# Graph attention, edge stage: GpSimd weighs one head of every pair of visits behind its gathers, TensorE lowers addresses ahead of its waits

## The reference

```python
Q, K, V = (x @ Wq), (x @ Wk), (x @ Wv)            # each reshaped to (N, 8 heads, 64)
score = jnp.einsum('ehd,ehd->eh', K[src], Q[dst]) / sqrt(64)
score = jnp.exp(jnp.clip(score, -5.0, 5.0))[..., None]
wV = segment_sum(V[src] * score, dst)
Z = segment_sum(score, dst)
h = x + (wV / (Z + 1e-06)).reshape(N, 512)
h = (h - mean(h)) * rsqrt(var(h) + 1e-05) * bn_gamma + bn_beta     # over the nodes
out = layernorm(x + h)                                            # over the features
```

## Time and profile before

| | us |
|---|---|
| three runs | 1913.06, 1907.57, 1913.44 |
| median | 1913.06 |
| the profiled execution | 1908.01 |
| its span in the trace | 1906.1 |

### The profile page before, as it was taken

One profiled execution on the slowest core, in us unless ns is written; L12 is line 12 of the kernel. 1 busy time (PEld: TensorE's weight loads), 2 busy tenths in 40 slices (PEclk: granted clock), 3 DMA queues, 4 the chain that ended last, 5 costly groups with the idle time before them and its releaser, 6 DMA issues.

```text
span 1906.1 us, 41424 instructions
## 1 busy us (share of the span) xinstructions
PE 1861.6 (98%) x7904; PEld 1362.2 (71%) x8014; DVE 1697.0 (89%) x2454; ACT 1367.5 (72%) x4602; POOL 1291.3 (68%) x1473
## 2 busy tenths in 40 slices
PE   7999999998999999999999999999999999999897
PEld 4555555554888888878888888888888888887333
DVE  6677755644999999999999999999999999999888
ACT  0002000002999999999999999999999999998857
POOL 0205666103777888788888888888888888885677
PEclk9999999999999999999999999999999999999999
DMA  5547788546999999999999999999999999999307
GB/s 183 162 151 250 288 319 274 186 161 231 357 358 356 362 367 358 346 351 368 368 356 353 352 366 369 354 355 355 366 361 358 360 355 365 370 358 370 122 33 287
DMA packets 184521, 589.09 MB, mean 309 GB/s; under 512 B 28480, under 2 KB 30240, under 8 KB 184480
## 3 DMA queue, kind: packets, MB, share of 16 engines
q0 software_dynamic: 135904, 465.14, 65.8%
q1 hardware_dynamic: 45120, 121.69, 17.8%
q10 hardware_dynamic: 3456, 1.78, 0.3%
HBM read 535.27 MB, written 78.91 MB: 322 GB/s over the span
## 4 chain that ended last, share of the span: by engine, by line
PE 74%; DVE 16%; issue 4%; DMA 4%; ACT 1%; POOL 1%; SPq 0%; DVEq 0%; ACTq 0%; POOLq 0%
PE acc L939 29%; PE places L342 22%; PE q_ps L923 17%; DVE kv L795 6%; DVE raw L806 5%; DMA kv<-kv_d,idx 2%; PE mm_ps L949 2%; PE banks L1151 1%; DVE stats L1288 1%; DVE agg L1281 1%; PE mm_ps L951 1%; PE places L402 1%; DMA q_tile<-xb_d 1%; POOL kv L751 1%; PE banks L1142 1%
## 5 line engine op out<-in xcount | busy, mean ns | idle before, releaser
L751 POOL DMA_INDIRECT kv<-kv_d,idx x880 | 887.0, 1008 | 339.2 <-issue 204.8
L846 ACT ACTIVATE kv<-kv 128x64 f32<-128x64 f32 x3520 | 889.0, 335 | 14.3
L939 PE MATMUL acc<-kv,mm_sb 128*128 128x260 f32 x3520 | 845.6, 383 | 4.1 <-POOL kv L714 2.2
L939 PEld LDWEIGHTS acc<-kv,mm_sb 128*128 128x128 f32 x3520 | 654.3, 190 | 137.9 <-issue 32.8
L923 PE MATMUL q_ps<-q_tile,mm_sb 128*128 x1760 | 559.2, 439 | 5.6 <-DVE kv L795 4.9
L795 DVE TENSOR_TENSOR kv<-q_ps,kv 128x1024 f32<-128x1024 f32 x440 | 536.1, 1218 | 14.0 <-PE q_ps L923 7.0
L806 DVE TENSOR_REDUCE raw<-kv 128x16 f32<-128x1024 f32 x440 | 532.2, 1210 | 0.0
L923 PEld LDWEIGHTS q_ps<-q_tile,mm_sb 128*128 128x128 f32 x1760 | 328.6, 189 | 74.4 <-DVE kv L795 20.8
L714 DVE TENSOR_TENSOR kv<-kv 128x384 f32<-128x384 f32 (+1 forms) x440 | 271.6, 617 | 0.1
L857 ACT ACTIVATE mm_sb<-mm_ps,less 128x1024 fp32r<-128x1024 f32 x220 | 241.2, 1096 | 13.1 <-remote 10.1
L435 ACT COPY p<-places 128x768 f32<-128x768 f32 x23 | 18.4, 798 | 243.5 <-PE places L342 243.5
(11 more groups left out here) (171 smaller groups left out, 1358.6 us busy)
## 6 DMA issues: line engine op xcount, KB each, us to landing
q_tile<-q_d SPq DMA_DIRECT2D x49, 512.0 KB, 7.2
kv<-kv_d,idx POOLq DMA_INDIRECT x880, 6.2
kv_d<-kv_a SPq DMA_DIRECT2D x25, 512.0 KB, 5.5
xb<-in_x POOLq DMA_DIRECT2D x49, 256.0 KB, 4.3
xb_d<-xb POOLq DMA_DIRECT2D x49, 256.0 KB, 3.7
out_rows<-agg SPq DMA_DIRECT2D x49, 256.0 KB, 2.1
x_sb<-in_xT SPq DMA_DIRECT2D x24, 512.0 KB, 7.9
q_d<-q_a SPq DMA_DIRECT2D x24, 512.0 KB, 4.1
```

The lines of the kernel that those rows point to most:

```text
L751: pool.indirect_dma_start(kv[:, s, u, 0:2 * DIM], None, kv_d, bass.IndirectOffsetOnAxis(idx[:, s, u:u + 1], 0), bounds_check=N_NODES - 1, ...
L846: return act.activation(v, v, ACT.Copy, scale=kv[:, s, u, 2 * DIM + h:2 * DIM + h + 1])
L939: last = pe.matmul(acc[:, bass.ds(par, 1), DIM - (1 - n) * HALF:DIM + n * HALF], m, kv[:, sc, u, DIM + n * HALF:DIM + (n + 1) * HALF], sta ...
```

## The change

Three things, all in `attend`:

1. GpSimd weighs head 7 of **every** pair, and in two instructions, one for each visit (`weigh_visit`, 64 values a partition). The first stands behind the gather of visit 0 (and behind the copy of row numbers, where there is one), the second behind the gather of visit 1. The wait for the exponentials, on `s_exp` of the pair five back, stands ahead of the first.
2. VectorE weighs three heads of every pair, none of four, and TensorE waits for three counts on `s_v` in every step.
3. TensorE's program works out the addresses of all four Q matmuls, and of all four sums, ahead of the waits in front of them (`pe.lower_ap`), as well as the values that `s_q` and `s_evict` are awaited with. In `follow`, `& 1` is written `% 2`.

```diff
-                return (mask >> k) & 1
+                return (mask >> k) % 2
...
+        def weigh_visit(eng, s, u):
+
+            first = HEADS - POOL_HEADS
+            v = kv[:, s, u, DIM + first * D_HEAD:2 * DIM]
+            w = kv[:, s, u, 2 * DIM + first:KVW].broadcast_to([P, D_HEAD])
+            return eng.tensor_tensor(v, v, w, ALU.mult)
...
+                if there(p):
+                    wait_apart(pool, s_exp[sp], fp)
+                    weigh_visit(pool, sp, 0)
                 if there(q):
                     gather(q, s, fills, 1)
-                if s % 2 and there(p):
-                    wait_apart(pool, s_exp[sp], fp)
-                    weigh(pool, sp, HEADS - POOL_HEADS, POOL_HEADS).then_inc(s_v[sp], 1)
+                if there(p):
+                    weigh_visit(pool, sp, 1).then_inc(s_v[sp], 1)
...
-                    weigh(dve, s2, ACT_HEADS, HEADS - ACT_HEADS - (POOL_HEADS if s % 2 == 0 else 0)).then_inc(s_v[s2], 1)
+                    weigh(dve, s2, ACT_HEADS, HEADS - ACT_HEADS - POOL_HEADS).then_inc(s_v[s2], 1)
...
+                    loaded = pe.snap(16 * (tiles[1] + 1), min_val=16, max_val=16 * TILES)
+                    parts = [q_tile[:, bass.ds(tiles[u] % 2, 1), n * DIM:(n + 1) * DIM].bitcast(F32R)
+                             for u in range(2) for n in range(2)]
+                    for part_q in parts:
+                        pe.lower_ap(part_q)
                     pe.wait_ge(s_mm[sb_ // 2], fb)
-                    pe.wait_ge(s_q, 16 * (tiles[1] + 1))
+                    pe.wait_ge(s_q, loaded)
                     for u in range(2):
                         for n in range(2):
-                            part_q = q_tile[:, bass.ds(tiles[u] % 2, 1), n * DIM:(n + 1) * DIM].bitcast(F32R)
+                            part_q = parts[2 * u + n]
...
-                    pe.wait_ge(s_v[sc], (2 if sc % 2 else 3) * fc)
-                    pe.wait_ge(s_evict, tiles[1] + 1)
+                    sums = [acc[:, bass.ds(tiles[u] % 2, 1), DIM - (1 - n) * HALF:DIM + n * HALF]
+                            for u in range(2) for n in range(2)]
+                    emptied = pe.snap(tiles[1] + 1, min_val=1, max_val=TILES)
+                    for part in sums:
+                        pe.lower_ap(part)
+                    pe.wait_ge(s_v[sc], 3 * fc)
+                    pe.wait_ge(s_evict, emptied)
```

More of the change, by code:

```diff
@@ L932, in step @@
                              for u in range(2)]
-                    pe.wait_ge(s_v[sc], (2 if sc % 2 else 3) * fc)
-                    pe.wait_ge(s_evict, tiles[1] + 1)
+                    sums = [acc[:, bass.ds(tiles[u] % 2, 1), DIM - (1 - n) * HALF:DIM + n * HALF]
[5 more added lines that the diff above has]
+                    pe.wait_ge(s_evict, emptied)
                     for u in range(2):
-                        par = tiles[u] % 2
                         m = one_hot(sc, u, 0).bitcast(F32)
                         for n in range(2):
-                            last = pe.matmul(acc[:, bass.ds(par, 1), DIM - (1 - n) * HALF:DIM + n * HALF], m,
+                            last = pe.matmul(sums[2 * u + n], m,
                                              kv[:, sc, u, DIM + n * HALF:DIM + (n + 1) * HALF],
```

## The result

The changed kernel takes 2078.57 us (median of four, 2077.04 to 2080.95) against 1910.99 us before (four runs, 1907.57 to 1913.44). The ratio is 1.0879, with a 95% interval of 1.0855 to 1.0904: 168 us slower, 8.8%. The forecast was 1959 us in a range of 1908 to 2000, and the measured time lies outside it. Its direction was right and the size was not: it foresaw 48 us and 168 came.

What follows compares the result with a forecast made beforehand. TensorE and VectorE bound the old kernel by a hair; GpSimd would bound the new one at 3.035 us a pair. (3.035 - 2.926) x 440 = 48 us on 1908.0, plus 3, gives 1959 us, range 1908 to 2000.

Steps and rivals of the forecast that it cites:

- The reading of the bound: Edge stage before: TensorE and VectorE bound by a hair; GpSimd nearly full, with 0.15 us a pair to give.
- the elastic weighing of the earlier trace: GpSimd's old 128-value weighing: 0.41 us undisturbed, mean 0.665, stretched when GpSimd runs ahead until it meets VectorE's weighing.
- The order of the waits: Edge stage after: GpSimd sets the pace, TensorE's sums wait for it, and VectorE's product waits for TensorE.
- the wait for the exponentials costs nothing: GpSimd's new wait in every step: ended long ago when GpSimd is late, so it costs 0.
- The line through 128 and 512 values: GpSimd visit size: 0.41 and 1.28 us give 2.27 ns a value, so 0.265 us for 64; 0.27 taken.
- The other reading that stood in the text: GpSimd visit of 64 values: with the copy's fixed part, near 0.30 us.
- the pauses and the gaps around the copy: GpSimd, per two pairs: pauses 0.04 us; the row-number copy with its gap adds 0.11 us.
- is a gain in itself: GpSimd: placing each visit behind a gather turns a gap of 0.30 into 0.18 us.
- So I take no stretch: GpSimd's visits: VectorE's weighing falls between them, in the second gather, so no stretch is added to 3.015 us a pair.
- The phase: Edge stage after: VectorE weighs about 1.6 to 2.6 us after a second visit's end, during the second gather (1.6 to 2.7).
- a rival of 0.08: GpSimd's visits meet VectorE's weighing and stretch: beyond 2000 us, 2044 with half the pairs caught; chance 0.08.
- TensorE's part: TensorE's address work ahead of the waits: costed at 0, with 3 us of gain or loss either way.

Runs made afterwards that it cites:

- The run with one input: Changed kernel with VectorE's two-input weighing of 3 heads replaced by a one-input reduction over the same 384 values; 1971.11 us, ratio 1.0324.

## Why the prediction was half right

**The reading of the bound held.** GpSimd, 68% busy by the page, had 0.15 us a pair to give and not the 18% of the earlier trace rows: one weighing for every pair, unstretched, took 2.96 us a pair, where GpSimd's own sum gave 2.97. Its idle pieces of 0.16 and 0.02 us stand unchanged around the shorter visits, as costs of an instruction. And the elastic weighing of the earlier trace rows is confirmed: with one input it takes 0.412 us and GpSimd idles instead.

**The order of the waits held**, as did that the wait for the exponentials costs nothing: GpSimd's idle time names ACT for 3.0 of 121.3 us.

**A visit was mis-sized by 0.03.** The line through 128 and 512 values gave 0.265 and I took 0.27; undisturbed it is 0.30. The other reading that stood in the text, a fixed part like that of the copy, was nearer: some 0.19 us. Two visits of a pair by 0.03 are 27 us of the sum. The run with one input, which has this and no stretch, came out at 1971, only 12 above the forecast of 1959; the pauses and the gaps around the copy came out smaller than forecast. That placing each visit behind a gather "is a gain in itself" holds for the gaps alone: the split as a whole cost 50 us.

**The step that failed is "So I take no stretch".** The phase was worked out right for some 60% of the pairs: it had VectorE weigh 1.6 to 2.6 us after the end of a second visit, in the time of the second gather. (In 135 of the 360 pairs in the middle VectorE weighs earlier, from the last part of the first gather on, and stretches neither gather.) In the trace after, a second visit ends at 1000.42, VectorE weighs from 1001.89 (1.47 later), the second gather starts at 1002.09 (1.67 later). But I took a gather to be immune, since no row that I read showed otherwise, and asked only whether a weighing would be caught. So the phase that looked safe was a bad one: the weighing stands on the start of 223 of 360 second gathers, and of nearly every copy. The forecast put the stretch into a rival of 0.08 and priced it for visits alone. The terms that were mis-sized, per pair: gathers 2 x 1.105 = 2.21 against 2.06 (+0.15), visits 0.64 against 0.54 (+0.10, of which 0.06 is the size of a visit above and 0.04 is stretch), the copy 0.12 against 0.05 (+0.07). Together +0.32, less 0.03 for pauses and gaps that came out smaller: 0.29 x 440 = 128 us, against the 120 by which the forecast missed.

A row in the trace before would have told me. These two stand beside each other in its timeline, the gather being the second after the pause in the earlier trace rows:

```profile
1063.47 0.55 DVE L714 TENSOR_TENSOR kv<-kv 128x384 f32<-128x384 f32 x1
...
1063.63 1.25 POOL L751 DMA_INDIRECT kv<-kv_d,idx  x1 [0.30 <-issue]
```

A gather of 1.25 us among hundreds of 0.99, starting inside VectorE's weighing. Only 20 of the 720 gathers in the middle of that stage begin so, and 13 of them take over 1.06 us; with the change 223 do. The pause of the earlier trace rows had pushed GpSimd out of its usual place and shown for one gather what the change then did to a third of them.

**TensorE's part** was costed at 0 within 3 us. Alone it gains 0.27%, 4 to 5 us, somewhat outside that bound. In the changed kernel it costs 41 us, which no price of the part itself could have shown.

**The page of the Trainium skill.** "SBUF — State Buffer", section "Who interferes with whom", has a VectorE instruction with two SBUF inputs contend with a GpSimd instruction that reads SBUF, and not one with a single input that runs outside its two-port modes. The runs with one input agree, with 1.029 against 1.105 us for a gather and 0.412 against 0.669 for the old weighing. The same section infers that `tensor_tensor` does not stall a DMA whose descriptors GpSimd generates. Here it lengthens GpSimd's gather instruction, 1.24 to 1.40 us in place of 1.02, when it stands on the gather's start; the measurement decides.

## What to carry to other kernels

Count an engine's fixed gaps and instruction starts as work before you give it more; a share of busy time of 68% can be a full engine, and an instruction that comes out short in one place may be elastic, paying out of slack that the change is about to spend. Where two engines share an access, list every kind of instruction of the one that could stand on the start of the other's, gathers and copies too, and look in the trace before for the few places where a pause has pushed them together: they show the price of a phase that the change may make permanent. And time the parts of a change apart: here a part that gained 0.27% by itself and parts that lost 6.8% without it (2037.6 us) stood in one diff, and in it the first made the rest worse by 41 us.

## What the runs showed of the hardware

A GpSimd instruction that begins while VectorE runs an instruction with two SBUF inputs is held until that instruction ends, but for its own first 0.15 us or so. It then ends at a fixed time behind VectorE's end. In the changed kernel this time is 0.043 us for the copy of 8 row numbers (95 of them), 0.145 for a visit of 64 values (55) and 0.90 for a gather (263), each within 0.02 us; in the kernel before it is 0.257 for the weighing of 128 values (169). Alone these instructions take 0.20, 0.30, 1.02 to 1.03 and 0.41 us, so that an overlap costs its own length less 0.12 to 0.16 us. The prediction had read the row of 0.77 us beside 0.51 as 0.7 us lost for each us of overlap; by these rows it is 0.51 + 0.26. For the overlaps of half a microsecond that count here the two prices are nearly the same.

What counts is that VectorE's instruction runs when GpSimd's begins. In the run with TensorE's part undone the weighing began 0.1 to 0.4 us into 143 gathers, and they took 1.03 us. There too the 22 gathers that began up to 29 ns behind the weighing's start took 1.03 us, and the 68 that began 31 to 60 ns behind it 1.39 us or more. With one SBUF input on VectorE's side neither gathers (163 met, 1.04 us) nor weighings of 128 values (273 met, 0.412 us) are held; no copy was met for 0.2 us or more in a run with one input.

In the other direction, VectorE's clip (`tensor_scalar`, SBUF to SBUF, 16 values) took 0.16 us alone. In the kernel with one weighing for every pair, the 387 clips that began 0.3 to 0.5 us into a gather took 0.56 us in the mean and ended 0.026 us before the gather did. In the kernel before, 204 clips began so far into a gather and took 0.165 us; one of them was held. What tells the two cases apart is open; no run was made for it.
